# Score passes of a graph kernel: rings of four, loads ahead and stores behind in SP's turn

## The reference

```
# attention, per layer l: scores of edges and of the loop at each node
h = (x @ Wg).reshape(n, HEADS, HID)
logits = leaky_relu(a_s[src] + a_d[dst] + ew)      # a_s, a_d: h times attention vectors
alpha = softmax of logits over the edges into a node
y = mean over heads of segment_sum(alpha * h[src], dst) + bias
x = relu(x + layer_norm(y))
# a block of the others, for a node that no edge enters:
z = x + relu(relu(x @ W1 + b1) @ W2 + b2)          # two-layer
z = x + relu(x @ W + b)                            # single
x = (z - mean(z)) * rsqrt(var(z) + eps)
```

## Time and profile before

| | us |
|---|---|
| runs (three) | 5644.61, 5651.83, 5657.78 |
| profiled execution, its own time | 5648.55 |
| its span, first to last instruction | 5646.7 |
| PE busy | 4247.3 (75%) |
| VectorE busy | 3979.2 (70%) |
| ScalarE busy | 3517.7 (62%) |
| GpSimd busy | 2496.2 (44%) |
| mean granted clock | 0.923 |
| pass 0, its first DMA to softmax's first | 1509.6 to 1957.0 |
| pass 1 | 2397.4 to 2750.5 |
| pass 2 | 3191.3 to 3650.2 |

### The profile page before, as it was taken

One profiled execution on the slowest core, in us unless ns is written; L12 is line 12 of the kernel. 1 busy time (PEld: TensorE's weight loads), 2 busy tenths in 40 slices (PEclk: granted clock), 3 DMA queues, 4 the chain that ended last, 5 costly groups with the idle time before them and its releaser, 6 DMA issues. The chain is left out here.

```text
span 5646.7 us, 108972 instructions
## 1 busy us (share of the span) xinstructions
PE 4247.3 (75%) x22666; PEld 2953.2 (52%) x22666; DVE 3979.2 (70%) x15056; ACT 3517.7 (62%) x11198; POOL 2496.2 (44%) x2510
## 2 busy tenths in 40 slices
PE   3777777767688759989499888759876768786664
PEld 2555555544466525566355566524365656675544
DVE  5777777777778777777777677789844868654433
ACT  1777777766577647778467677648833767522222
POOL 2555555520144212255222344201176767676777
PEclk9999999989899979999799999979999999998777
DMA  2445555549799737689467699736654656554332
GB/s 74 153 157 162 162 159 157 157 152 314 255 294 297 252 108 229 215 287 308 145 193 229 219 293 291 248 112 227 208 156 146 213 183 213 166 158 128 91 98 75
DMA packets 617508, 1084.53 MB, mean 192 GB/s; under 512 B 105692, under 2 KB 131806, under 8 KB 617384
## 3 DMA queue, kind: packets, MB, share of 16 engines
q1 hardware_dynamic: 541928, 957.57, 50.6%
q0 software_dynamic: 75456, 125.65, 9.4%
HBM read 620.55 MB, written 466.24 MB: 192 GB/s over the span
## 5 line engine op out<-in xcount | busy, mean ns | idle before, releaser
L2195 POOL DMA_INDIRECT got_c<-table,src_row x980 | 931.3, 950 | 379.1 <-issue 296.8
L1233 POOL DMA_INDIRECT src_got_s<-table,src_row x588 | 554.6, 943 | 942.5 <-DVE delta_s L1471 486.9
L1783 POOL TENSOR_TENSOR part_m<-part_m,half_sum_m 128x512 f32<-128x512 f32 x147 | 220.9, 1503 | 1114.3 <-DVE half_sum_m L1997 1114.3
L2220 PE MATMUL bank<-pick_c,got_c 128*128 128x128 f32 x1960 | 327.1, 319 | 396.7 <-DMA got_c<-table,src_row 349.9
L1792 PE MATMUL bank<-w_all,dt_m 128*128 128x512 f32 x1176 | 569.0, 601 | 21.4 <-DMA dt_m<-delta_t 19.9
L2220 PEld LDWEIGHTS bank<-pick_c,got_c 128*128 128x128 f32 x1960 | 282.2, 222 | 439.0 <-issue 311.5
L1385 ACT ACTIVATE z_s<-z_s,shift_s,dev_s 128x128 f32<-128x128 f32 x1176 | 482.7, 483 | 4.6 <-DVE shift_s L1504 1.9
L2319 ACT COPY agg_c<-bank 128x512 f32<-128x512 f32 x245 | 143.4, 585 | 517.6 <-DVE bank L1633 286.4
L713 PEld LDWEIGHTS bank<-w_mean,ht 128*128 128x128 f32 x2352 | 346.2, 212 | 164.2 <-issue 164.2
L686 POOL DMA_INDIRECT raw_half<-in_x_dram,dst_node x196 | 204.7, 1044 | 492.5 <-PE bank L744 373.2
L710 PE MATMUL bank<-bias,first_row 128*128 128x512 f32 x588 | 353.6, 686 | 59.1 <-DVE rows L838 30.1
(11 more groups left out here) (310 smaller groups left out, 11854.6 us busy)
## 6 DMA issues: line engine op xcount, KB each, us to landing
table<-rows SPq DMA_DIRECT2D x294, 256.0 KB, 3.8
x_s<-table SPq DMA_DIRECT2D x294, 256.0 KB
x_c<-table SPq DMA_DIRECT2D x245, 256.0 KB
table<-mid_s SPq DMA_DIRECT2D x196, 256.0 KB
table<-z_s SPq DMA_DIRECT2D x196, 256.0 KB
table<-z_c SPq DMA_DIRECT2D x196, 256.0 KB
own_rows_s<-table SPq DMA_DIRECT2D x147, 256.0 KB
pick_t_s<-picks_t SPq DMA_DIRECT2D x147, 256.0 KB
```

Of the source, the lines that this page charges most:

```text
L1233: nc.gpsimd.indirect_dma_start(out=src_got[r][:, g, :], out_offset=None, in_=tables[l].rows, in_offset=bass.IndirectOffsetOnAxis(ap=src_ro ...
L1783: nc.gpsimd.tensor_tensor(flat(part[r]), flat(part[r]), flat(half_sum[r]), ALU.add).then_inc(parts_added, 1)
L2195: nc.gpsimd.indirect_dma_start(out=got[r][:, g, :], out_offset=None, in_=t_in.rows, in_offset=bass.IndirectOffsetOnAxis(ap=src_row[:, t:t ...
L2220: ins = nc.tensor.matmul(b_sum[r][:, k * P:(k + 1) * P], got[b.slot][:, k, :], pick[r][:, k, :], start=k == 0, stop=sage, skip_group_check ...
```

## The change

Only `edge_scores` changes.

1. `src_got`, `own_rows`, `pick_t`, `dt`, `x`, `z` and `mid` become rings of four, with four semaphores each; batch b uses slot b % 4. `delta`, `scores`, `xt`, `ht` and the small tiles stay at two.
2. The holds move two batches back: x, own, picks and gathers wait for batch b-4, and `residual`, `middle` and `delta_out` for the stores of b-4.
3. SP's step is put in another order, all loads of batch n first, then the stores of n-4 and n-5. Its lag goes from 4 to 5.
4. All four streams (SP, PE, ACT, DVE) use loop bodies of four steps instead of two. The order on PE, ACT and DVE stays.
5. The node rows of batches 0 and 1 are loaded before SP waits for the tile ends.

```diff
-                src_got, own_rows, pick_t, delta, dt = (pairs(n) for n in ("src_got", "own_rows", "pick_t", "delta", "dt"))
+                def fours(name):
+                    return [s(f"{name}{r}", [P, GB, D]) for r in range(4)]
+                src_got, own_rows, pick_t, dt = (fours(n) for n in ("src_got", "own_rows", "pick_t", "dt"))
+                delta = pairs("delta")
-                x, z = ([pairs(f"{n}{h}_") for h in range(2)] for n in ("x", "z"))
+                x, z = ([fours(f"{n}{h}_") for h in range(2)] for n in ("x", "z"))
...
                         def load_rows(b, h):
                             n = b.twin(h)
-                            hold(sp, z_read, n.count(1, -3))
+                            hold(sp, z_read, n.count(1, -7))
                         def load_own(b):
-                            hold(sp, spread_made, b.count(1, -1))
+                            hold(sp, spread_made, b.count(1, -3))
...
+                        for c in range(2):
+                            load_rows(Batch(0, c, 4), 0)
+                            load_rows(Batch(0, c, 4), 1)
                         if l:
                             sp.wait_ge(tails_in, 16 * n_tails)
...
+                        def loads(b):
+                            load_own(b)
+                            load_picks(b)
+                            if not early(b):
+                                load_rows(b, 0)
+                                load_rows(b, 1)
+
                         def step_two(at):
+                            b = at(0)
+                            if b:
+                                loads(b)
                             b = at(4)
                             if b:
+                                store_middle(b, 0)
+                                store_middle(b, 1)
+                                store_delta(b)
                                 store_score(b)
+                            b = at(5)
+                            if b:
+                                store_rows(b, 0)
+                                store_rows(b, 1)
+
+                        def step_one(at):
+                            b = at(0)
+                            if b:
+                                loads(b)
                             b = at(4)
                             if b:
+                                store_rows(b, 0)
                                 store_rows(b, 1)
+                            b = at(5)
                             if b:
                                 store_delta(b)
                                 store_score(b)
-                        skewed(sp, nb, 4, step_two if first else step_one)
+                        skewed(sp, nb, 5, step_two if first else step_one, 4)
...
-                            r = b % 2
-                            if b > 1:
-                                pool.wait_ge(delta_made, b - 1)
+                            r = b % 4
+                            if b > 3:
+                                pool.wait_ge(delta_made, b - 3)
...
-                            hold(dve, z_stored[h][b.half], b.ring(16, -16))
+                            hold(dve, z_stored[h][b.slot], b.ring4(16, -16))
```

More of the change, by code:

```diff
@@ L1075, in edge_scores @@
                 if first:
-                    ht, mid, b1 = pairs("ht"), [pairs(f"mid{h}_") for h in range(2)], s("b1", [P, 1])
+                    ht, mid, b1 = pairs("ht"), [fours(f"mid{h}_") for h in range(2)], s("b1", [P, 1])
                 stat6, stat = s("stat6", [P, GB, 6]), pairs("stat", (P, GB, 2))
@@ L1109, in _, with load_rows, load_own @@
                             sp.dma_start(b1[:, :], first[1]).then_inc(w_in, 16)
+                        def load_rows(b, h):
+                            n = b.twin(h)
+                            hold(sp, z_read, n.count(1, -7))
+                            sp.sem_inc(sp_pace, 1)
+                            sp.dma_start(flat(x[h][b.slot]), batch_rows(t_in.nodes, n.batch())).then_inc(x_in[h][b.slot], 16)
+                        def load_own(b):
+                            hold(sp, spread_made, b.count(1, -3))
+                            sp.sem_inc(sp_pace, 1)
+                            sp.dma_start(flat(own_rows[b.slot]), batch_rows(tables[l].slots, b.batch())).then_inc(own_in[b.slot], 16)
@@ new lines, in load_picks, with store_middle @@
+                        def load_picks(b):
+                            hold(sp, spread_made, b.count(1, -3))
+                            sp.sem_inc(sp_pace, 1)
+                            sp.dma_start(flat(pick_t[b.slot]), turned_batch(picks_t, b)).then_inc(pick_in[b.slot], 16)
+                        def store_middle(b, h):
+                            n = b.twin(h)
+                            sp.wait_ge(mid_made, n.count(1, 1))
+                            sp.sem_inc(sp_pace, 1)
+                            sp.dma_start(batch_rows(t_mid.nodes, n.batch()), flat(mid[h][b.slot])).then_inc(mid_stored[h][b.slot], 16)
@@ new lines, in store_rows, with store_delta @@
+                        def store_rows(b, h):
+                            n = b.twin(h)
+                            sp.wait_ge(z_made, n.count(1, 1))
+                            sp.sem_inc(sp_pace, 1)
+                            sp.dma_start(batch_rows(t_out.nodes, n.batch()), flat(z[h][b.slot])).then_inc(z_stored[h][b.slot], 16)
+                        def store_delta(b):
+                            sp.wait_ge(dt_made, b.count(1, 1))
+                            sp.sem_inc(sp_pace, 1)
+                            sp.dma_start(turned_batch(delta_t, b), flat(dt[b.slot])).then_inc(dt_stored[b.slot], 16)
@@ new lines, in store_score, with early @@
+                        def store_score(b):
+                            sp.wait_ge(sig_out, b.count(1, 1))
+                            sp.sem_inc(sp_pace, 1)
+                            sp.dma_start(edge_score[:, bass.ds(b.batch() * (GB * P), GB * P)], scores[b.half][:, :]).then_inc(sc_stored[b.half], 16)
+                        def early(b):
+                            return isinstance(b.i, int) and b.batch() < 2
+                        for c in range(2):
+                            load_rows(Batch(0, c, 4), 0)
+                            load_rows(Batch(0, c, 4), 1)
@@ L1476, in middle @@
                             dve.wait_ge(h_turned, n.count(1, 1))
-                            hold(dve, mid_stored[h][b.half], b.ring(16, -16))
-                            nc.vector.tensor_copy(flat(mid[h][b.half]), bank[3][:, :]).then_inc(mid_made, 1)
+                            hold(dve, mid_stored[h][b.slot], b.ring4(16, -16))
+                            nc.vector.tensor_copy(flat(mid[h][b.slot]), bank[3][:, :]).then_inc(mid_made, 1)
                         def residual(b, h):
@@ L1490, in moments @@
                             for g in range(GB):
-                                ins = nc.vector.bn_stats(stat6[:, g, :], z[h][b.half][:, g, :])
+                                ins = nc.vector.bn_stats(stat6[:, g, :], z[h][b.slot][:, g, :])
                             ins.then_inc(z_moments, 1)
```

118 lines of the change are left out of this document (27 added, 91 removed).

## The result

The changed kernel takes 5481.18 us (median of five runs, 5479.18 to 5486.81) against 5651.83: ratio 0.9702 (of the means), 95% interval 0.9688 to 0.9716. That is 170.6 us less; the prediction had 110 less (5542, range 5505 to 5612). The time lies outside the range, on the good side. (One execution of the kernel before took 10264.52 us; the comparison leaves it out.)

The account below looks back on a forecast made before the run. It took the loop through z's store at ring depth two as the bound, not PE or DMA; beats gave 40.3 + 45.1 + 19.7, lead-ins 5, together 110 us off 5648.55, plus 3.3 for the median: 5542 us, range 5505 to 5612.

Parts of the forecast that it names:

- The z loop: Two-layer passes: ring depth two on z's store sets the beat; VectorE's 1.37 and PE's 0.94 us a batch go.
- What is late next is PE itself at 7.81: Two-layer passes: with the store wait gone, PE's busy time of 7.81 us a batch sets the beat.
- VectorE (7.07) is under PE: Two-layer passes: without the store wait VectorE needs 7.07 us a batch, less than PE's 7.81.
- Beats 7.95 and 6.35: Forecast us a batch in two-layer passes and pass 1, from 8.79, 8.89 and 6.76; gains 40.3, 45.1 and 19.7 us.
- DMA: Rival: today's cost per byte bounds beats at 8.12 and 6.38 us, 5560 us total; chance 0.23 together with scores.
- TensorE waiting for x in pass 1: Pass 1: loads asked for 2 to 3 beats ahead remove 16.7 us of PE waits for node rows.
- Scores: Pass 1: ring left at two is the tightest wait; if it binds, beat stays 6.76; chance 0.23 together with DMA-bound.
- Lead-ins: Before each pass's first difference: early node rows gain 4 us in pass 1, 1 in pass 2, 0 in pass 0.
- The drain: Behind the last batch of a pass: unchanged, since SP then only waits for data.
- Loop bodies: Four-step bodies taken to cost nothing; rival: code fetched at each turn costs 104 us, 5646 total; chance 0.05.
- The price of 3.46 us a turn: Loop-body rival: each of 30 turns costs 3.46 us, read from ACT's stop between two phases; 104 us in all.
- The range: Total time 5505 to 5612 us: down to the first-beat pace of 7.5 without quite reaching it, up past 5593.

Follow-up runs that it names:

- f2: Kernel before with loop bodies of four and four slots for z alone, SP's old order; 5530.02 us, ratio 0.9785 to the kernel before.
- h1: Changed kernel with three quarters of each VectorE bias copy left out inside the loop; 5479.52 us.
- e7: Changed kernel with scores in a ring of four; 5482.52 us, ratio 0.9689 to the kernel before.
- e8: Changed kernel with scores in a ring of four and early rows issued between the tile-end stores and the wait for them; 5475.95 us, ratio 0.9688.
- f4: Changed kernel without the node rows loaded ahead of the tile ends; 5490.24 us, ratio 0.9717 to the kernel before.
- e1: Kernel before with loop bodies of four, all rings still two, SP's old order; 6252.15 us, ratio 0.9963 to the kernel before.
- g2: Changed kernel with 15/16 of the picks load left out inside the loop, 246 of 2610 KB a batch; 5480.29 us.
- h3: Changed kernel with three quarters of the bias copies and of the score matmul and 15/16 of the picks load left out; 5466.33 us.
- h2: Changed kernel with three quarters of the VectorE bias copies and of the TensorE score matmul left out; 5473.34 us.

## Why the prediction was wrong

- **The z loop: right.** The 1.37 us wait on VectorE and TensorE's 0.94 for `delta` went to zero, and f2 shows that the z ring carries most of the gain.
- **"What is late next is PE itself at 7.81": the step that failed.** 7.81 was busy time per batch in a stretch where TensorE kept stopping. A matmul's row is longer than the distance to the next start (0.60 and 1.02 us long, 0.44 and 0.86 to the next start), so before each stop a tail counts as busy in which the next matmul could have started. Start to start, the trace of before already had the numbers, in its timeline of TensorE:

```profile
1744.47 0.60 PE L1263 MATMUL bank<-ident,ht_s 128*128 128x128 f32 x4
1744.91 1.02 PE L1256 MATMUL bank<-xt_s,w_s 128*128 128x512 f32 x2
1745.77 1.05 PE L1292 MATMUL bank<-own_rows_s,pick_t_s 128*128 128x128 f32 x8
1746.66 1.02 PE L1306 MATMUL bank<-dt_s,w_sig 128*128 128x512 f32 x2
1747.52 1.05 PE L1279 MATMUL bank<-w_s,ht_s 128*128 128x128 f32 x8
```

  Four transposes take 0.44, a 512-column product 0.86, eight small ones 0.89. A batch, with `turn_rows` as two times four transposes, is 0.88 + 2 x 0.89 + 2 x 0.44 + 2 x 0.86 + 0.89 + 0.86 + 0.44 = 7.45; h1 measured 7.44. In pass 1 the busy time said 6.20; the same distances, with the 0.86 of a bias matmul and without `hidden` and `turn_hidden`, give 5.71, and the beats of e7 and e8 are 5.73 and 5.70. The Trainium skill, "Perfetto Trace Analysis", section "Identifying the Most-Contended Engine", says that matmul busy time is no good measure of closeness to the roofline because the instructions are pipelined and look smaller in the trace. The trace agrees that the measure misleads, but here it erred the other way: busy time overstated the work by 0.37 us a batch.
- **"VectorE (7.07) is under PE": wrong.** Its busy time left out the waits for itself, 10.5 us in 34 batches, and 2.3 us before starts. All of VectorE's time but the wait that goes is (300 - 46.6)/34 = 7.45, and it became the bound, at 7.50. The same page calls occupancy a fair measure for this engine; in this trace it stood at 95% when the engine was full. Taking the removed wait off the beat, 8.79 - 1.37, 6.76 - 0.86 (25.2/29.25) and, by the wait of 50.7 us in 33.75 batches of pass 2, 8.89 - 1.50, would have given 7.42, 5.90 and 7.39 and a gain of 179 us; measured 177. That the sum is so near is partly luck: two of these beats are 0.07 and 0.10 too low and one 0.13 too high. What I took as TensorE's floor, and the margin for DMA on top of it, left 105 of the 179.
- **Beats 7.95 and 6.35** came out at 7.49 and 5.77: 105 us forecast, 177 measured. This is the whole of the miss; the lead-ins went the other way.
- **DMA: right in direction.** The same bytes now cost (85.8 + 14.9)% x 300/40 = 7.55 us a batch, not 8.12, at 351 GB/s. But neither figure was a floor: in the two-layer passes no run that cut bytes got faster by more than 0.03 us a batch. The 23% for that rival and `scores` were too many, since a share near one was read as fullness.
- **TensorE waiting for x in pass 1: right**, 16.7 us to 0.2. **Scores: right and small**, 11.1 us in 35.5 batches of pass 1, which e7 removes.
- **Lead-ins: wrong.** Forecast were gains of 4, 1 and 0 us in passes 1, 2 and 0; measured 0.0, -2.5 and +0.1. First DMA to first `difference` is 20.92 and 21.10 us in passes 1 and 2. The node rows are asked for early, but the gathered tile ends then land later. SP's early rows, its tile-end stores and its first load behind them in pass 2:

```profile
3087.54 1.79 SPq L1118 DMA_DIRECT2D x_s<-table  x4
3092.79 1.42 SPq L1162 DMA_DIRECT2D table<-tails_s  x2
3096.88 0.34 SPq L1123 DMA_DIRECT2D own_rows_s<-table  x1
```

  From the pass's first DMA at 3085.66 to the first load behind the mended slots are 11.2 us, where the kernel before took 8.9 (3191.25 to 3200.18). f4, without the early rows, takes 9.0 in both passes, so it is they that cost the 2.2. The price of 0 to 1 us in the prediction was too small. The drain was not "unchanged" either: the end of pass 1 took another 2.1 (last `difference` to `softmax`'s first DMA, 7.76 to 9.91); in passes 0 and 2 it stayed at 13.7 to 13.8.
- **Loop bodies: right.** There were eight packets of instructions in 40 batches, no wait put down to them, and e1 no slower. (The price of 3.46 us a turn was read from a wait at the barrier between phases, ended by TensorE's sequencer; that it is the cost of new code no row shows.)
- **The range.** Its low end, 5505, rested on a beat of 7.5 as something not quite reached, though the earlier trace rows showed 7.54 run with all slots free. One first interval is a weak measure (in the changed kernel the first four are 7.38, 7.73, 7.44 and 7.48), but it was near 7.49 and I set it aside.
- **A reading of the earlier trace rows:** of the slices named as about 0.9 busy, 14 and 26 stand at 7 and slice 20 at 4. Nothing was worked out from them.

## What to carry to other kernels

When a change removes one wait in a steady loop, first take that wait off the beat on the engine that has it. With all its self-inflicted idle time kept, the rest is an estimate of that engine's own time a turn, good to 0.13 us a batch here. For TensorE take start-to-start distances from a stretch without stops, not busy time. And deepen the ring before moving a store later: the new order and early rows, worth 21 us with four slots for z, left the kernel 241 us slower than before with two.

## What the runs showed of the hardware

- A DMA share of 1.00 to 1.02 wasn't saturation in the two-layer passes: cutting 9% of the bytes left the beat at 7.50 (g2) and 7.39 (h3 beside h2). The rates went to 357 GB/s in two-layer passes (h2) and 367 in pass 1 (e7).
- The DMA time of the same bytes is not fixed: 8.12 us a batch before, 7.55 after. It isn't only that the loads were asked for earlier: f2, with SP's old order and all rings but z's at two, has (83.9 + 14.6)% of a beat of 7.88, 7.76 us. And where 9% of the direct bytes were left out (g2), the same gathers went from 14.9 to 17.4% (1560:1860). The cause stays open.
- On one occasion the same program took 6277 us instead of 5652, and the gain of a ring (2.1%) shrank to 0.3% there.
